# Loading the images of a small vision tower in 24 transfers of 96 partitions, with the position rows and their sum moved

## The reference, cut to what matters

```
patches = x.reshape(b, c, 6, 16, 6, 16).transpose(0, 2, 4, 1, 3, 5)   # -> (b, 36, 768)
tok = patches @ W_emb + b_emb;  tok = concat([cls0, tok]) + pos_embedding
h = concat([cls_tok, tok])                                            # (16, 38, 192)
h = h + attn(layernorm(h));  h = h + ffn(layernorm(h))
```

## Time and profile before

| | us |
|---|---|
| median of 3 runs | 267.15 |
| lowest and highest | 264.56, 270.74 |
| the profiled execution's own time | 268.69 |
| its span | 266.9 |
| PE busy | 223.2 (84%) |
| DVE busy | 150.5 (56%) |
| ACT busy | 110.5 (41%) |
| POOL busy | 73.7 (28%) |

### The profile page before, as it was taken

One profiled execution on the slowest core, in us unless ns is written; L12 is line 12 of the kernel. 1 busy time (PEld: TensorE's weight loads), 2 busy tenths in 40 slices (PEclk: granted clock), 3 DMA queues, 4 the chain that ended last, 5 costly groups with the idle time before them and its releaser, 6 DMA issues.

```text
span 266.9 us, 4475 instructions
## 1 busy us (share of the span) xinstructions
PE 223.2 (84%) x1340; PEld 191.6 (72%) x1340; DVE 150.5 (56%) x464; ACT 110.5 (41%) x252; POOL 73.7 (28%) x103
## 2 busy tenths in 40 slices
PE   6379699796999999998989955189999999999950
PEld 6268399564697967876767752079999999999940
DVE  5234318859476957858575688756768443433300
ACT  2343463767133453726242478035433342424210
POOL 4001260073305050414221335001324242423330
PEclk9658659799799999999985555559999999999995
DMA  7999999999400000000101298351333334341213
GB/s 121 132 233 172 235 287 271 266 225 289 123 10 0 0 4 1 2 0 0 29 2 26 56 324 205 80 136 42 70 47 59 47 54 52 52 55 18 29 15 85
DMA packets 26259, 25.73 MB, mean 96 GB/s; under 512 B 4970, under 2 KB 23261, under 8 KB 26221
## 3 DMA queue, kind: packets, MB, share of 16 engines
q1 hardware_dynamic: 22333, 22.16, 35.1%
q0 software_dynamic: 3568, 2.64, 7.8%
q10 hardware_dynamic: 336, 0.66, 1.7%
HBM read 16.56 MB, written 7.77 MB: 91 GB/s over the span
## 4 chain that ended last, share of the span: by engine, by line
PE 62%; DVE 14%; DMA 11%; issue 4%; ACT 3%; POOL 2%; SPq 2%; DVEq 0%; POOLq 0%; ACTq 0%
PE ps L950 11%; PE ps L973 10%; PE ps L580 5%; PE ps L708 4%; DMA wemb<-in_L_tok_W_emb 4%; DMA sums<-ys,xs 4%; PE ps L798 4%; PE ps L712 4%; PE ps L784 4%; PE ps L677 3%; PE ps L962 3%; PE ps L691 2%; DMA sent<-row,index 2%; SPq L428 1%; POOL sent L1612 1%
## 5 line engine op out<-in xcount | busy, mean ns | idle before, releaser
L1648 POOL DMA_INDIRECT sums<-ys,xs x17 | 26.3, 1546 | 67.0 <-ACT ys L1548 60.7
L973 PE MATMUL ps<-w2s,hidT 128*128 x204 | 36.1, 327 | 1.1 <-DVE hidT L1352 0.8
L973 PEld LDWEIGHTS ps<-w2s,hidT 128*128 128x128 f32 x204 | 33.2, 189 | 2.0 <-issue 1.6
L950 PE MATMUL ps<-w1hi,xhi 128*128 x68 | 25.3, 372 | 1.4 <-DVE xhi L1332 0.8
L1548 ACT ACTIVATE ys<-ps,xs 128x192 f32<-128x192 f32 x17 | 7.2, 421 | 40.0 <-PE ps L973 37.6
L1331 DVE TENSOR_TENSOR xlo<-ps,xhi 128x128 fp32r<-128x128 f32 x17 | 5.0, 292 | 29.8 <-ACT xend L1541 29.8
L784 PE MATMUL ps<-vm,ktok 114*96 114x288 f32 (+1 forms) x48 | 15.6, 406 | 5.0 <-DVE kvb L1147 5.0
L1635 POOL COPY vexp<-vtok 114x32 f32<-114x32 f32 (+1 forms) x36 | 8.0, 222 | 41.4 <-PE ps L712 39.5
L1430 ACT ACTIVATE qlb<-ps,cst 96x228 f32<-96x228 f32 (+1 forms) x36 | 12.1, 425 | 17.2 <-PE ps L746 17.2
L1612 POOL DMA_INDIRECT sent<-row,index x12 | 13.5, 1128 | 18.1 <-DVE row L1219 14.8
L708 PE MATMUL ps<-at,vexp 114*96 114x114 f32 (+1 forms) x144 | 18.2, 281 | 0.0
(11 more groups left out here) (197 smaller groups left out, 486.3 us busy)
## 6 DMA issues: line engine op xcount, KB each, us to landing
w2s<-in_L_ffn_W SPq DMA_DIRECT2D x8, 576.0 KB, 8.0
sent<-blank SPq DMA_DIRECT2D x1, 3977.0 KB, 32.3
w1s<-in_L_ffn_W SPq DMA_DIRECT2D x4, 768.0 KB, 17.1
xs<-sent SPq DMA_DIRECT2D x17, 96.0 KB, 1.9
w1s<-in_L_ffn_W SPq DMA_DIRECT2D x4, 384.0 KB, 18.5
w1hi<-w1hi SPq DMA_DIRECT2D x8, 192.0 KB, 3.9
ximg<-in_x SPq DMA_DIRECT2D x12, 96.0 KB, 9.3
w1s<-in_L_ffn_b SPq DMA_DIRECT2D x1, 792.0 KB
```

What stands on the lines that cost most here:

```text
L950: last = pe.matmul(ps[2 + c][:, 0:PASS], xx, of_expert(ww, expert), start=(n == 0), stop=(n == len(products) - 1))
L973: last = pe.matmul(ps[6 + j % 2][:, 0:D], hidT[:, k, :], of_expert(w2s[:, :, k, :], expert), start=(k == 0), stop=(k == FCH - 1))
L1648: po.indirect_dma_start(sums, bass.IndirectOffsetOnAxis(ap=xs[:, j % NS, D + TAIL + 1:].bitcast(U32), axis=0), ys[:, j % 2, :], None, comp ...
```

## The change

Each channel comes in 8 transfers instead of 6 (`PIECES`): a transfer takes 2 of the 16 pixel rows of all six grid rows and all 16 images, so 96 partitions with 768 bytes in a row for each. SP issues the even pieces, ACT the odd ones. The source has three levels, grid row (6), image (16), 192 numbers. The first load of the constants takes 114 columns more (`EARLY` = 242), since `repeat` now stands behind the identity. The loads of the position rows go from SP's queue to the head of POOL's, with the wait for DVE's memset. PE forms the base behind turn 3, ACT copies it to `hbase` between channel 1 and channel 2. The wait for the rest of the constants goes to the first `key_sums`.

```diff
@@ CONSTS: "repeat" directly behind "ident"; EARLY = 128 + GTOK; PIECES = 8
-        def load_rows(engine, c, i):
-            engine.dma_start(ximg[i * IMAGES:(i + 1) * IMAGES, c].rearrange("p y w -> p (y w)"),
-                             x.rearrange("b c (i y) w -> c i b (y w)", y=PATCH)[c, i]).then_inc(x_in[c], 16)
+        def load_rows(engine, c, k):
+            rows = slice(k * PATCH // PIECES, (k + 1) * PATCH // PIECES)
+            engine.dma_start(ximg[:, c, rows, :].rearrange("p y w -> p (y w)"),
+                             x.rearrange("b c (i y) w -> c i b y w", y=PATCH)[c][:, :, rows, :].rearrange(
+                                 "i b y w -> i b (y w)")).then_inc(x_in[c], 16)
@@ sync
-                for i in range(GRID):
-                    if i % 3 < 2:
-                        load_rows(sp, c, i)
-            sp.dma_start(cst[:, 128:], consts[:, 128:]).then_inc(consts_in, 16)
-            sp.wait_ge(dv_posb_zero, 1)
-            sp.dma_start(posa[0:1, :], ...).then_inc(pos_in, 16)     # and three more, L478 to L480
+                for k in range(0, PIECES, 2):
+                    load_rows(sp, c, k)
+            sp.dma_start(cst[:, EARLY:], consts[:, EARLY:]).then_inc(consts_in, 16)
@@ tensor
+            def base():
+                pe.wait_ge(pos_in, 64)
+                for k, part in enumerate((posa, posb)):
+                    last = pe.matmul(ps[5][0:GTOK, 0:D], const("repeat"), part[:], start=(k == 0), stop=(k == 1))
+                last.then_inc(pe_base, 1)
             for k in range(KCH):
                 turn_patches(k)
+                if k == 3:
+                    base()
                 if k >= 2:
                     first_parts(k - 2)
             first_parts(KCH - 2)
             first_parts(KCH - 1)
-            pe.wait_ge(consts_in, 16)
-            pe.wait_ge(pos_in, 64)
-            for k, part in enumerate((posa, posb)): ...
@@ key_sums, group 0
+                    pe.wait_ge(consts_in, 16)
@@ scalar
-            ac.dma_start(cst[:, 0:128], consts[:, 0:128]).then_inc(ident_in, 16)
+            ac.dma_start(cst[:, 0:EARLY], consts[:, 0:EARLY]).then_inc(ident_in, 16)
             for c in range(CH):
-                for i in range(GRID):
-                    if i % 3 == 2:
-                        load_rows(ac, c, i)
+                for k in range(1, PIECES, 2):
+                    load_rows(ac, c, k)
...
+                if c == 1:
+                    ac.wait_ge(pe_base, 1)
+                    ac.activation(hbase[:], ps[5][0:GTOK, 0:D], ACT.Copy).then_inc(ac_base, 1)
@@ gpsimd, ahead of its first load
+            po.wait_ge(dv_posb_zero, 1)
+            po.dma_start(posa[0:1, :], ...).then_inc(pos_in, 16)     # and three more
```

More of the change, by code:

```diff
@@ L65 @@
 WARM = 10
+PIECES = 8
 HEAD = 128
@@ L84 @@
     "ident": (128, 128),
+    "repeat": (SEQ, GTOK),
     "band": (GTOK + 1, GTOK),
@@ L93 @@
     "number": (128, GROUPS + 1),
-    "repeat": (SEQ, GTOK),
     "expert": (1, E),
@@ L104 @@
 CONST_COLS = _at
+EARLY = 128 + GTOK
 def constants():
@@ L484, in _ @@
             sp.dma_start(b2s[:], b2).then_inc(wg_in, 16)
-            sp.wait_ge(x_in[CH - 1], 16 * GRID)
+            sp.wait_ge(x_in[CH - 1], 16 * PIECES)
             sp.wait_ge(wemb_in, 16)
@@ L600, in _ @@
             first_parts(KCH - 1)
-            pe.wait_ge(consts_in, 16)
-            pe.wait_ge(pos_in, 64)
-            for k, part in enumerate((posa, posb)):
-                last = pe.matmul(ps[5][0:GTOK, 0:D], const("repeat"), part[:], start=(k == 0), stop=(k == 1))
-            last.then_inc(pe_base, 1)
             def turn_projections():
@@ L1026, in _ @@
             for c in range(CH):
-                ve.wait_ge(x_in[c], 16 * GRID)
+                ve.wait_ge(x_in[c], 16 * PIECES)
                 ve.tensor_copy(patch_rows(c, 0), image_rows(c, 0)).then_inc(dv_patch_rows, 1)
@@ L1369, in _ @@
             for c in range(CH):
-                ac.wait_ge(x_in[c], 16 * GRID)
+                ac.wait_ge(x_in[c], 16 * PIECES)
                 ac.activation(patch_rows(c, 1), image_rows(c, 1), ACT.Copy).then_inc(ac_patch_rows, 1)
@@ L1378, in _ @@
             ac.activation(anc[2][:], anc[1][:], ACT.Exp).then_inc(ac_anchor_exp, 1)
-            ac.wait_ge(pe_base, 1)
-            ac.activation(hbase[:], ps[5][0:GTOK, 0:D], ACT.Copy).then_inc(ac_base, 1)
             ac.wait_ge(dv_eps, 1)
@@ L1574, in _ @@
             linked = {}
+            po.wait_ge(dv_posb_zero, 1)
+            po.dma_start(posa[0:1, :], cls_tok.rearrange("a b d -> (a b) d")).then_inc(pos_in, 16)
+            po.dma_start(posa[1:SEQ, :], pos_emb[0]).then_inc(pos_in, 16)
+            po.dma_start(posb[1:2, :], cls0.rearrange("a b d -> (a b) d")).then_inc(pos_in, 16)
+            po.dma_start(posb[2:SEQ, :], b_emb.partition_broadcast(SEQ - 2)).then_inc(pos_in, 16)
             for k, w in enumerate((w_loc, w_str, w_glo)):
```

## The result

The changed kernel takes 272.26 us (median of 4 runs, 271.82 to 272.7). The kernel before, run beside it on the same chip, took 268.27 (4 runs, 264.56 to 270.74). The ratio is 1.0241, with a 95% interval of 1.0151 to 1.033: slower, clear of noise, though the interval does not settle whether by more than 2%.

The account below looks back on a forecast made before the run. PE was taken as the bound, its embedding work starting when the matrix lands. An earlier matrix, less the base put ahead of the blend, gave -0.25 us: profiled 268.4, median 266.9 us, range 262.6 to 269.9.

Parts of the forecast that it names:

- Six engines: New image transfers: source outer count 6 and target 96 share divisor 6, so six of 16 DMA engines work.
- the old form itself is slow: Image loads before the change: 6144 bytes into each of 16 neighbouring partitions move at only 141 GB/s, against 336 elsewhere.
- When the data lands: Start of the kernel: at 120 to 129 GB/s the embedding matrix lands at 15.7 us instead of 16.15.
- Rival 2: Image loading: six engines at 104 GB/s or ACT stalled; matrix at 18.0 us, total 268.2 to 269.7 us; chance 0.22.
- ACT's queue: ACT's 12 image issues at 0.47 us each, plus a stall and the table load: ACT ready at 10.5 us.
- The base in the middle: PE, behind turn 3: base takes 1.31 us at half clock instead of 0.85; turn 5 ends at 23.5 us.
- The rest: POOL's loads cost nothing, SP's `qkvw` is wanted at 25.45 us, the moved constants wait is free.
- The blend is what is late next: Before `h`: the 2.0 us blend, behind DVE's last patch copy, ends at 25.85 us; `h` starts at 25.9.
- A shift goes through to the end whole: Behind `h` nothing changes, so the 0.25 us gained there reaches the kernel's end in full.
- my exception: Behind `h`: a shift moving a stretch against the clock; a rise 3 us earlier or later worth 1.5 us.
- The sum: Whole kernel: 0.25 us gained, between 0.15 lost and 0.6 gained; median 266.9 us.
- The chances: Whole kernel: forecast 0.42, three rivals 0.23, 0.22, 0.13; faster than 261.8 us 0.10, slower than 272.5 us 0.06.

Follow-up runs that it names:

- e3: The changed kernel with image-tile partitions ordered image by image (16 x 6) instead of grid row by grid row, for 16 engines; median 267.97 us, ratio to before 0.9989.
- e6: The changed kernel with image-by-image partitions (16 engines), 4 pieces per channel and the base behind the last parts; median 267.1 us, ratio to before 1.0066.
- e5: The changed kernel with all of POOL's loads held until channel 0 is in; median 271.69 us, ratio to before 1.023.
- e4: The changed kernel with 4 pieces per channel: 12 transfers of twice the size, still six engines; median 271.91 us, ratio to before 1.0167.
- e10: The changed kernel with the old image transfers and all of POOL's loads held until channel 0 is in; 271.2 us (1 run).
- e7: The changed kernel with the base back behind parts 5 and ACT's copy behind the blend's exponents; median 273.63 us, ratio to before 1.0304.

## Why the prediction was wrong

**Six engines**: right, by the share of 0.41 and by e3. That the old form itself is slow was right too: from 5.5 to 9 us the kernel before moved 141 GB/s with its engines counted as busy, e3 202 and e6 245 with the new form on all 16.

**When the data lands**: this step failed. It gave the six engines 120 to 129 GB/s, the two higher of the three values of the earlier trace rows, and `wemb` at 15.7 us; it landed at 19.11. The bytes that I had counted ahead of it, 1629 KB or 1.668 MB, took 17.1 us from 2.0 on: 98 GB/s in the mean, by stretches 112 and then 77. Rival 2 had taken 104 and 18.0 us. The direction of rival 2 was right, its size too small by 1.1 us. Two reasons for the error are visible. In the earlier trace rows 120 GB/s at a share of 0.39 is 308 GB/s for a full share of 1; here it is 112 / 0.41 = 273. And from 5.5 to 9 us the six engines were not even busy (0.28 of 0.375). POOL's loads may have a part in that, since with them held back (e5) the share was 0.40 there; how large it is isn't shown.

**ACT's queue**: mis-sized. I took 0.47 us an issue and a stall; the shortest issue took 0.72 us and all twelve 10.69, so ACT was ready at 13.2 instead of 10.5. With all 16 engines (e3), the source again in three levels, one took 0.57 to 0.71, most of them 0.62; so about 0.1 us of the 0.72 goes with the six engines, and the rest above 0.43 with the form of the transfer. The section of the Trainium skill named above says that for fewer than 16 engines the issuing sequencer itself writes the rest of the semaphore's count. That may be the 0.1 us; no run here shows it. I had priced a late ACT at half to one for one. e4, with ACT's issues done 5.6 us earlier, shows that the matrix hides it.

**The base in the middle**: this step failed as well, by two errors. The base took 1.55 us and not 1.31, and so did parts 1 behind it; and I let the clock rise at 22.6 us by the clock on the wall, though parts 0 was to move, and though the base would stand in that stretch. It rose at 28.7. Parts 2, turn 5 and all up to it ran at half clock, and the blend behind them moved with them. In the single profiles this is 1.09 us of the 4.05 at `h`, the other 2.96 being the matrix.

**The rest** held in the main. POOL's position rows were in time and PE never waited for the base's rows in the kernel after; in e10, where they were held back, it did, until 18.18 us. `qkvw` landed 11.4 us behind its issue and held nothing up. The blend is what is late next, and its counterpart above. "A shift goes through to the end whole" held for the change itself (240.7 against 240.8) but not for e7: my exception, a stretch moved against the clock, was worth 2.6 us there.

**The sum.** The time is 5.4 us above the forecast. The kernel after is 4.0 slower than before where I had 0.25 gained, and 1.1 is the kernel before itself, whose median was 267.15 when I forecast and 268.27 with the fourth run.

**The chances**: slower, past 272.5 us, had 0.06, on the ground that it needed rival 2 and a second stretch at half clock; 272.26 is just short of that line. Rival 2's own mechanism turned out larger than its bound, and more half clock came with it, in the embedding itself.

## What to carry to other kernels

Before a transfer is reshaped for its target's partitions, look at the outer dimension of its source: 6 x 16 rows of 96 partitions went over six engines, 16 x 6 rows over all 16, and that alone was worth 4.3 us in the medians (272.26 to 267.97). When a rate is taken from another stretch, take the low row for a sum that a whole stage waits for, and put the high one in the range. A time at which the clock rises belongs to the work ahead of it, so move it with that work, add what you put in, and leave room for its scatter (3.1 and 6.2 us behind parts 0 in two profiles of one kernel).

## What was unexpected of the hardware

- An issue of an image transfer took mostly 0.43 us in the old form (partitions by 6144 bytes), 0.57 to 0.71 in the three-level form over 16 engines, and 0.72 at the least over six.
- Six engines moved 77 GB/s in one stretch of 3.5 us, and 141 in another (20 to 22 us) of the same kernel.
- The same kernel's `h` came at 26.14 and at 23.54 us in two profiles, with its data 1.5 us apart and the clock's rise 4.6 us apart.
- The fall of the clock in the attention stage came in two places from kernel to kernel, and the earlier one went with 2 to 3 us more behind `h`, with the same instructions in that stage.
